# Both halves of the ninth tile's shared expert become late halves: a fused time-mix, channel-mix and mixture-of-experts kernel

## What is computed

```
x = x + attn(layernorm(x))      # time mix: a scan over 512 tokens; channel mix: F = 512
h = layernorm(x)                # 8192 tokens
logits = h @ router_w.T         # 16 experts, top 1
routed = expert(h * sigmoid(top logit))          # 128 -> 2*128 -> 128, one of 16
shared = silu(h @ gate.T) * (h @ up.T) @ down.T  # 128 -> 512 -> 128, every token
out = x + routed + shared
```

## Time and profile before

| | us |
|---|---|
| median of 3 runs | 490.42 (490.4 to 490.5) |
| profiled execution, span from first to last instruction | 510.8 |
| profiled execution's own time beside the span | not given |
| rounds 12, 13, 14 (T1 to T1) | 19.56, 25.62, 19.55 |
| turns 0 to 39 | 125.05 |
| end, from there | 30.2 |

### The profile page before, as it was taken

One profiled execution on the slowest core, in us unless ns is written; L12 is line 12 of the kernel. 1 busy time (PEld: TensorE's weight loads), 2 busy tenths in 40 slices (PEclk: granted clock), 3 DMA queues, 4 the chain that ended last, 5 costly groups with the idle time before them and its releaser, 6 DMA issues.

```text
span 510.8 us, 10511 instructions
## 1 busy us (share of the span) xinstructions
PE 485.5 (95%) x3093; PEld 391.8 (77%) x3093; DVE 368.8 (72%) x1056; ACT 320.9 (63%) x623; POOL 353.3 (69%) x573
## 2 busy tenths in 40 slices
PE   8899999999999999999999999989999899899777
PEld 6665777777777777868678678778998788779766
DVE  6979999999999999978999896473443443344415
ACT  3576897897897887876879865533544453345212
POOL 6656599889889889876888776762365566556650
PEclk9999999999999999999999999999999999999989
DMA  6015010110110101101011011114886444440027
GB/s 227 3 39 230 21 37 28 62 33 32 62 32 33 62 22 43 62 21 44 22 42 43 1 42 43 43 41 126 205 221 169 125 122 124 125 115 20 23 80 251
DMA packets 33031, 39.33 MB, mean 77 GB/s; under 512 B 4913, under 2 KB 29113, under 8 KB 32720
## 3 DMA queue, kind: packets, MB, share of 16 engines
q1 hardware_dynamic: 26640, 24.98, 16.8%
q0 software_dynamic: 5760, 13.16, 7.4%
q10 hardware_dynamic: 576, 0.52, 0.3%
HBM read 21.69 MB, written 17.93 MB: 78 GB/s over the span
## 4 chain that ended last, share of the span: by engine, by line
PE 76%; DVE 7%; issue 6%; ACT 3%; another core or an unknown queue 3%; POOL 2%; DMA 2%; SPq 0%; DVEq 0%; ACTq 0%; POOLq 0%
PE bank L427 17%; PE bank L420 9%; PE bank L444 6%; PE bank L414 4%; PE bank L435 4%; PE bank L815 3%; PE bank L823 3%; PE bank L822 3%; PE bank L528 3%; PE bank L514 3%; PE bank L540 3%; PE bank L519 3%; PE bank L524 3%; PE bank L688 2%
## 5 line engine op out<-in xcount | busy, mean ns | idle before, releaser
L427 PE MATMUL bank<-hT,wm 128*128 128x256 f32 x512 | 125.9, 385 | 3.3 <-issue 2.7
L427 PEld LDWEIGHTS bank<-hT,wm 128*128 128x128 f32 x512 | 92.6, 192 | 22.2 <-issue 12.1
L1610 POOL DMA_INDIRECT out<-shared x55 | 53.9, 979 | 52.1 <-DVE shared L1442 25.6
L1528 POOL DMA_INDIRECT sorted_rows<-rows,posi x64 | 72.3, 1130 | 19.7 <-issue 16.9
L420 PEld LDWEIGHTS bank<-wm,k 128*128 128x128 f32 x512 | 61.7, 192 | 7.6 <-issue 6.6
L420 PE MATMUL bank<-wm,k 128*128 128x128 f32 x512 | 62.1, 276 | 0.0
L1084 ACT ACTIVATE er<-bank 128x256 f32<-128x256 f32 x40 | 15.3, 383 | 47.5 <-remote 24.3
L1442 DVE TENSOR_TENSOR shared<-bank,shared 128x256 f32<-128x256 f32 x28 | 11.8, 420 | 32.4 <-remote 17.4
L1610 POOL DMA_INDIRECT out<-rows x24 | 23.5, 978 | 14.5 <-issue 8.0
L444 PE MATMUL bank<-wm,actA 128*128 128x128 f32 x240 | 32.9, 281 | 0.0
L944 ACT ACTIVATE h<-rows,smE 128x128 f32<-128x128 f32 x64 | 26.3, 482 | 8.9 <-POOL smE L1504 8.9
(11 more groups left out here) (256 smaller groups left out, 1308.0 us busy)
## 6 DMA issues: line engine op xcount, KB each, us to landing
shared<-sorted_rows SPq DMA_DIRECT2D x56, 128.5 KB
shared<-x SPq DMA_DIRECT2D x16, 256.0 KB
rows<-sorted_rows SPq DMA_DIRECT2D x24, 128.5 KB
wexp<-w_exp SPq DMA_DIRECT2D x2, 1536.0 KB, 8.2
sorted_rows<-filler SPq DMA_DIRECT2D x17, 128.5 KB
shared<-out SPq DMA_DIRECT2D x6, 256.0 KB
out<-shared SPq DMA_DIRECT2D x12, 128.0 KB, 2.2
sorted_rows<-rows,posi POOLq DMA_INDIRECT x64
```

What stands on the lines that cost most here:

```text
L427: ins = mm(dst[:, j * HALF:(j + 1) * HALF], W(name, 2 * pair_ + j), src[:, half * HALF:(half + 1) * HALF], start=True, stop=True)
L1528: g_.indirect_dma_start(sorted_ap, bass.IndirectOffsetOnAxis(posi[t % 3][:, g:g + 1].bitcast(U32), 0), rows[t % 3][:, g, :], None).then_in ...
L1610: g_.indirect_dma_start(out, bass.IndirectOffsetOnAxis(xr[k % RING][:, j, D:D + 1].bitcast(U32), 0), xr[k % RING][:, j, D + 1:ROW], None, ...
```

## The change

Tile 8 leaves `A_TILES`, and `B_TILES` with all that belongs to it is taken out: PE's second-half products and the waits on their semaphores, two Silus on ACT, two products and an add on DVE. Both halves of tile 8 enter `LATE` as units 8 and 9, and the later units move up by two. There are now 18 late halves: three in the `C_TILES` slots, 15 in the turns. The last sixteen steps stay sixteen, so 41 steps are spread over turns 4 to 39. The late sums get one more buffer (`kr[2]`). The rows of the ninth pair of halves are loaded into `xa[0]` by one more load on SP, with a semaphore of its own. The halves that DVE adds in the last of three places are 8 to 15 instead of 8 to 13.

```diff
-A_TILES, B_TILES, C_TILES = (0, 1, 2, 3, 4, 5, 6, 7, 8, 9, 10, 11, 12, 13, 14), (8,), (13, 14, 15)
-LATE = [(0, 1), (1, 1), (2, 1), (3, 1), (4, 1), (5, 1), (6, 1), (7, 1), (9, 1), (10, 1), (11, 1), (12, 1), (13, 1), (14, 1), (15, 0), (15, 1)]
+A_TILES, C_TILES = (0, 1, 2, 3, 4, 5, 6, 7, 9, 10, 11, 12, 13, 14), (13, 14, 15)
+LATE = [(0, 1), (1, 1), (2, 1), (3, 1), (4, 1), (5, 1), (6, 1), (7, 1), (8, 0), (8, 1), (9, 1), (10, 1), (11, 1), (12, 1), (13, 1), (14, 1), (15, 0), (15, 1)]
...
-        late_to = xn1tok + xn1T + ew + kr[0:2]
+        late_to = xn1tok + xn1T + ew + kr[0:3]
...
-        SP_LOADS, GP_LOADS = [0, 2, 4, 6, 8, 14], [10, 12]
+        SP_LOADS, GP_LOADS = [0, 2, 4, 6, 8, 14, 16], [10, 12]
...
+        def tl_pair(u):
+            return shared[:, u * HALF:(u + 2) * HALF] if u < 16 else xa[u // 2 - 8][:, :]
+
         def tl_of(u):
-            return shared[:, u * HALF:(u + 1) * HALF]
+            return tl_pair(u // 2 * 2)[:, u % 2 * HALF:(u % 2 + 1) * HALF]
...
+            if u >= 16:
+                return "tl_more", 0
...
-                for t in at(5, B_TILES):
-                    wait(pe, "hT", t)
-                    wait(pe, "sg0", t)
-                    unit_product(bank[2], "gate", 0, hT[t % HR], 1).then_inc(s["hG0"], 1)
...
-                for t in at(5, B_TILES):
-                    wait(pe, "hT", t)
-                    wait(pe, "sg1", t)
-                    unit_product(bank[4], "gate", 1, hT[t % HR], 1).then_inc(s["hG1"], 1)
-                    wait(pe, "hT", t)
-                    wait(pe, "ac0", t)
-                    unit_product(bank[3], "up", 0, hT[t % HR], 1).then_inc(s["hU0"], 1)
...
-                for t in at(5, B_TILES):
-                    wait(pe, "hT", t)
-                    wait(pe, "kr3", t + 2)
-                    unit_product(bank[5], "up", 1, hT[t % HR], 1).then_inc(s["hU1"], 1)
...
-                for t in at(5, B_TILES):
-                    wait(pe, "hac0", t)
-                    wait(pe, "base", t)
-                    unit_down(ACC, actB[0], 0, 1).then_inc(s["hD0"], 1)
...
-                for t in at(5, B_TILES):
-                    wait(pe, "hac1", t)
-                    unit_down(ACC, actB[1], 1, 1).then_inc(s["hD1"], 1)
...
-                for t in at(6, B_TILES):
-                    wait(act_e, "hG0", t)
-                    wait(act_e, "hac0", t - 1)
-                    af(sgB[0][:, :], bank[2][:, :], ACT.Silu).then_inc(s["hsg0"], 1)
...
-                for t in at(6, B_TILES):
-                    wait(dve, "hD1", t)
-                    v.tensor_tensor(base_of(t)[:, 2:4, :], by_group(ACC)[:, 2:4, :],
-                                    base_of(t)[:, 2:4, :], ALU.add).then_inc(s["hbase"], 1)
...
-                    wait(gp, "hbase", t)
                     wait(gp, "hs", t)
                     wait(gp, "posi", t)
                     if g < 2 and t in A_TILES:
-                        gp.wait_ge(s["base"], t + 1)
+                        gp.wait_ge(s["base"], A_TILES.index(t) + 1)
```

More of the change, by code:

```diff
@@ L72 @@
     hT=1, LG=1, lgt=1, mx=1, oh0=1, cm=2, oh=1, ths=1, sc=1, hs=1, RK=1, prk=1, reg=1, pmk=1, posf=1,
-    posi=1, G0=1, U0=1, sg0=1, ac0=1, G1=1, U1=1, sg1=1, ac1=1, D1=1, base=1, hG0=1, hU0=1, hsg0=1, hac0=1,
-    hD0=1, hG1=1, hU1=1, hsg1=1, hac1=1, hD1=1, hbase=1, cG0=1, cU0=1, csg0=1, cac0=1, cD0=1, cG1=1, cU1=1,
+    posi=1, G0=1, U0=1, sg0=1, ac0=1, G1=1, U1=1, sg1=1, ac1=1, D1=1, base=1,
+    cG0=1, cU0=1, csg0=1, cac0=1, cD0=1, cG1=1, cU1=1,
     csg1=1, cac1=1, cD1=1, cbase=1,
@@ L81 @@
     WHO[_n] = A_TILES
-for _n in ("hG0", "hU0", "hsg0", "hac0", "hD0", "hG1", "hU1", "hsg1", "hac1", "hD1", "hbase"):
-    WHO[_n] = B_TILES
 for _n in ("cG0", "cU0", "csg0", "cac0", "cD0", "cG1", "cU1", "csg1", "cac1", "cD1", "cbase"):
@@ L108, in program @@
                   *(f"x_in{i}" for i in range(XR)), *(f"scat{i}" for i in range(3)),
-                  *(f"{n}{i}" for n in ("xr_in", "xout") for i in range(8)), "tl_out", "tl_add", "tl_in"):
+                  *(f"{n}{i}" for n in ("xr_in", "xout") for i in range(8)), "tl_out", "tl_add", "tl_in", "tl_more"):
             s[n] = ctx.enter_context(nc.semaphore(n))
@@ L338, in load_late @@
                 a0, a1 = first_row(u) // HALF, first_row(u + 1) // HALF
-                eng.dma_start(shared[:, u * HALF:(u + 2) * HALF].rearrange("p (h c) -> p h c", h=2),
+                eng.dma_start(tl_pair(u).rearrange("p (h c) -> p h c", h=2),
                               halves_[:, a0:a1 + 1:a1 - a0, :]).then_inc(s[tl_sem(u)[0]], 16)
@@ L510, in keys @@
                     pe.wait_ge(s["w_in1"], 16)
-                wait(pe, "hsg0", t - 2)
                 wait(pe, "sg0", t - 2)
@@ L515, in keys @@
                 wait(pe, "xn2T", t)
-                wait(pe, "hsg1", t - 2)
                 wait(pe, "sg1", t - 2)
@@ L520, in keys @@
                 wait(pe, "xn2T", t)
-                wait(pe, "hac0", t - 2)
                 wait(pe, "ac0", t - 2)
@@ L580, in v_product @@
                 wait(pe, "xn1T", t)
-                wait(pe, "hac1", t - 4)
                 wait(pe, "kr3", t - 2)
@@ L632, in value_first @@
                 wait(pe, "k20", t)
-                wait(pe, "hbase", t - 2)
                 wait(pe, "base", t - 2)
@@ L851, in late_step @@
                         wait(act_e, f"cac{step}", NT)
-                        wait(act_e, f"hac{step}", NT)
                     af(late_sg(u)[step][:, :], late_bank(u, step)[0][:, :], ACT.Silu).then_inc(s["lsg"], 1)
@@ L978, in one_round @@
                     af(xn1T[t % 2][:, :], T1_B[:, :], ACT.Identity, bias=V("b1"), scale=V("g1")).then_inc(s["xn1T"], 1)
-                for t in at(6, B_TILES):
-                    wait(act_e, "hG1", t)
-                    wait(act_e, "hac1", t - 1)
-                    af(sgB[1][:, :], bank[4][:, :], ACT.Silu).then_inc(s["hsg1"], 1)
                 for t in at(4):
@@ L1304, in one_round @@
                     bn_stats_of(stC[t % 2], lambda g: grp(a[t % 2], g), "agC")
[L1305 to L1308, removed]
                 for t in at(3):
@@ L1349, in one_round @@
                     v.reciprocal(grp(q[t % 2], 1), grp(q[t % 2], 1))
[L1350 to L1353, removed]
                 for t in at(5, A_TILES):
@@ L1416, in late_step @@
                         wait(dve, f"cD{step}", NT)
-                        wait(dve, f"hD{step}", NT)
                     v.tensor_tensor(late_act(u)[step][:, :], late_sg(u)[step][:, :], late_bank(u, step)[1][:, :], ALU.mult).then_inc(s["lac"], 1)
```

## The result

| | time, us | ratio to before (95%) |
|---|---|---|
| before | 490.41 | |
| after, four executions | 496.61 (495.00 to 498.06) | 1.0121 (1.0105 to 1.0137) |
| after, five more | 496.98 (495.44 to 498.29) | 1.0128 (1.0109 to 1.0148) |
| forecast | 494.5 (490.2 to 496.8) | |

Slower, as forecast, and 2.1 us more than forecast: close to the time of the rival in which the clock falls in round 13 (496.2). The profiled execution took 498.06, with a span of 496.2. First its stretches: rounds 12, 13 and 14 (T1 to T1), the turns from first to last scatter, and the end from the first late load on; columns as in the earlier trace rows, to which these lines answer.

The account below looks back on a forecast made before the run. The prediction took PE to bound both the rounds and the turns, so moving its work gains nothing by itself. Rounds -7.3, turns +10.7 and end +0.7 make +4.1 on 490.42: 494.5 us, range 490.2 to 496.8.

Parts of the forecast that it names:

- the rival in which the clock falls in round 13: PE's new wait in round 13 drops its clock, adding 1.7 us to the forecast: 496.2 us; chance 0.20.
- The second half, -6.06: Round 13: the second half's work and waits stood there alone, so removing them saves 6.06 us.
- The first half, "-1.3": Rounds 12 and 13: of 5.24 us PE work removed only 1.3 returns; POOL's chain makes PE wait about 2.8.
- The choice between 1.41 and 2.30 for the scaling: Round 13, POOL's row scaling: at 1.41 us the first half returns 1.3 us, at 2.30 only 0.4; 1.3 taken.
- if the granted clock drops in the rounds: One of the prediction's stated signs of being wrong: PE's granted clock falling in the rounds.
- PE flows on: Rounds: POOL's chain does not hold PE, so both halves return in full, -11.3 us: 490.5 us, no difference; chance 0.13.
- The turns, "+10.7": Turns of the routed experts: four more gate/up steps and four more down steps add 10.7 us of PE work.
- upper end of 11.6: Turns: upper end of the added time, 10.7 us plus the same share of gaps, 11.0 over 114.
- The gaps of the turns: Turns: 11.0 us of idle PE in the profile, none counted as filled, since full turns have gaps too.
- PE gaps unchanged near 11 us: Turns: a sign of being right, that idle PE time there stays near 11 us after the change.
- The end, "+0.7": End: DVE adds two more halves, 0.355 us each, ahead of the last stores: +0.7 us, with ends 0 and +1.9.
- the end costs more: End: the ninth pair's load and stores are not hidden, 1.9 us instead of 0.7: 495.7 us; chance 0.08.

Follow-up runs that it names:

- e4: Of the change only tile 8's second half becomes late, its first half staying in the rounds (17 late halves): 488.88 us, against 490.72 for the kernel before on the same chip.
- e1: Changed kernel plus 12 spare matmuls that yield nothing, ahead of the transposes of h in round 13, to keep PE busy in its wait: 494.59 us.
- e0: The kernel before, profiled a second time with no edit: 490.64 us, span 488.5.
- e9: The changed kernel run again with no edit, five more executions: 496.98 us.
- e2: Changed kernel with both late halves of tile 8 left out entirely (steps, load, adds and stores): 484.21 us.
- e8: Changed kernel with the receptance product Wr (two matmuls) put ahead of the transposes of h in round 13, into PE's wait: 495.47 us.
- e3: Changed kernel with POOL's first-norm statistics of tile 13 moved behind the four q products in round 13: 496.12 us.
- e7: On top of e3, ACT instead of POOL scales tile 8's rows, and row_ids of tile 10 goes behind the q products: 494.36 us.
- e5: On top of e1, the adds of late units 8 and 9 cover one column instead of 256; load and stores stay: 494.26 us.
- e6: On top of e1, late units 8 and 9 have no load and no stores; the adds stay: 492.80 us.

## Why the prediction was right, and where it was off

**The second half, -6.06.** Right: e4 shows 25.62 becoming 19.55, without a new wait.

**The first half, "-1.3".** The mechanism was right, the size too high: with the clock kept (e1) the rounds lose 6.87, so the first half returned 0.8. That PE's wait is 2.82 as worked out is luck in part, for two errors cancel. PE was expected at the transposes at 219.3 and came at 220.04; h was expected at 222.1 and came at 222.81. Of each difference 0.29 is only that this trace's rounds start later (T1 of tile 4 at 57.57 against 57.28); 0.45 and 0.42 are left. For h the cause is in POOL's and DVE's timelines:

```profile
218.66 1.08 POOL L1442 TENSOR_SCALAR smE<-mvE 128x4 f32<-128x4 f32 x1
219.83 1.02 POOL L1444 TENSOR_TENSOR smE<-smE,half 128x4 f32<-128x4 f32 x1
220.93 0.20 POOL L1458 TENSOR_TENSOR smE<-smE 128x4 f32<-128x4 f32 x1
...
221.39 1.41 POOL L1468 TENSOR_SCALAR rows<-h,sc 128x128 f32<-128x128 f32 x4
```
```profile
218.60 1.16 DVE L1316 TENSOR_TENSOR_SCAN num<-decay,ev 128x512 f32<-128x512 f32 x1
```

An operation that takes 0.19 in e4 took 1.08: it began 0.06 after DVE's scan and ended 0.02 before the scan's end. DVE, freed of its products, reached the scan 2.2 us earlier than in e0 (218.60 against 220.82), while the round itself began 1.4 earlier; so the scan now meets smE. The choice between 1.41 and 2.30 for the scaling was right, and the scan is its likely reason as well: before, it began 0.22 after the scaling did.

**The clock: a rival at 0.20, and it came.** This is the step that failed: "the forecast leaves it out". The one gap of that length in the profile had brought the fall, the forecast's own wait was as long, and at least four of nine executions had it. It costs 1.5 to 2.4 us in the rounds (priced at 1.7). The prediction's own sign of being wrong, "if the granted clock drops in the rounds", has come true; the time is inside the range because the range's upper end was laid over this rival, not because leaving the clock out was right. With it the change of the first half makes the rounds longer, not shorter: 215.88 and 216.79 against e4's 215.19. The traces show the fall at waits of 2.82 us (after, e9, e2) and of 1.97 us (e8), while waits of 1.44 (e3, e7) left the clock up in the profiled executions (one other execution of e3 shows 0.992). The Trainium skill, "TensorE: Matmul & The Clock Gate", section "HAM oscillation — how this bites in real kernels", tells of the clock falling in waits between bursts of matmuls, but in longer waits than these; here the measurements decide.

**PE flows on.** Refuted: the wait is there, and e3 and e7 show two further limits behind POOL's order, its scatter's landing and DVE's statistics for h's norm.

**The turns, "+10.7".** Right: 10.03 (after), 10.93 (e1) and 11.27 (e9). (Its upper end of 11.6 comes to 11.7 by its own terms.) The two executions of the same program differ by 1.2, so that e4's 4.69 for one half against 5.34 says nothing more.

**The gaps of the turns.** That none would be filled was right, for a wrong reason: there were none (e0). "PE gaps unchanged near 11 us" is refuted.

**The end, "+0.7".** Put on the wrong work: without the adds nothing is gained (e5), without the transfers 1.5 us (e6). That is the rival "the end costs more", priced at 1.9 in all. The tail behind PE's last matmul grew by 0.6 (e1), 1.05 (e9) and 2.1 (after), so the forecast's size and the rival's both lie in its spread.

Together: with the clock kept, e1 has a median of 494.59 (493.78 to 495.51), and the two executions of the changed kernel at 0.998 took 495.00 and 495.44; by e1 the forecast's sum of 494.5 holds. With the fall the medians are 496.6 to 497.0. What stays open is why the end varies so much between executions with the same bytes. In the profiled one the last 2.2 us are almost empty:

```profile
491.00:492.00 1.00, 0.00 (x0) 0.00 (x0) 0.00 (x0) 0.00 (x0) 0.00 (x0) 0.89 1.10 381
...
494.00:495.00 1.00, 0.00 (x0) 0.00 (x0) 0.00 (x0) 0.00 (x0) 0.00 (x0) 0.50 0.07 24
495.00:496.20 1.20, 0.00 (x0) 0.00 (x0) 0.00 (x0) 0.00 (x0) 0.00 (x0) 0.50 0.03 9
```

A share of 0.03 to 0.07 of 16 engines is, as an estimate, the work of about one of them (1/16 is 0.06).

## What to carry to other kernels

When PE bounds a stage, giving part of its work away pays only up to the point where the next chain stands; past it the same work is paid in full elsewhere and the slack becomes a wait. Moving the half whose removal left an ordinary round gained 0.3%; moving the other one as well cost some 1.6%. New waits of 1.97 and 2.82 us on a PE that is otherwise busy came with the clock's fall in all four profiles of them (2.82 in after, e9 and e2, 1.97 in e8), so such a wait is to be priced with the fall behind it, as the likely case. And a stretch of gaps in a profile whose span is far above the median should be looked for in a second execution before an argument rests on it.

## What the hardware showed that was not expected

**POOL behind DVE's scan.** In round 13 of after, e1, e3, e4 and e7 a small POOL operation begins during DVE's scan (1.16 us), and ends with it. In e4 the product L1461 took 0.56 instead of 0.20:

```profile
218.96 1.02 POOL L1447 TENSOR_TENSOR smE<-smE,half 128x4 f32<-128x4 f32 x1
220.06 0.56 POOL L1461 TENSOR_TENSOR smE<-smE 128x4 f32<-128x4 f32 x1
```
```profile
219.47 1.16 DVE L1319 TENSOR_TENSOR_SCAN num<-decay,ev 128x512 f32<-128x512 f32 x1
```

It ended at 220.62, the scan at 220.63. The Trainium skill, "SBUF — State Buffer", section "Who interferes with whom", says that a VectorE instruction with two inputs in SBUF contends with a GpSimd instruction that reads SBUF, and calls the ports that the two engines share an exclusive lock. The scan reads two such inputs, decay and ev, and the traces agree, to 0.02 us, for a POOL operation that begins during the scan. The other order shows no wait here: the pow L1447 had begun 0.51 us before the scan in e4, and neither took longer than elsewhere (1.02 and 1.16 us).

**The clock after a wait.** The grant can fall when PE is already at work again: in e9 it fell some 0.9 us after the wait of 2.82 had ended, and in e2 1.7 us after it; both were low for some 3.4 us. In after it fell during the wait and was low for 6.83.
